# Two cross-attentions written out as one stage of eight head groups, on one Trainium2 core

## The reference, cut to what matters

```python
def _cross_attention(q_in, kv_in, wq, bq, wk, bk, wv, bv, wo, bo, bias_k, bias_v):
    qh = (q_in @ wq + bq).reshape(b, q_len, H, K)          # q_in = layer_norm(x), H = 16, K = 128
    kh = (kv_in @ wk + bk).reshape(b, t, H, K)             # t = 64
    vh = (kv_in @ wv + bv).reshape(b, t, H, K)
    kh = concatenate([kh, bias_k]); vh = concatenate([vh, bias_v])
    logits = einsum('bqhk,bthk->bhqt', qh, kh) / sqrt(K)
    ctx = einsum('bhqt,bthk->bqhk', softmax(logits), vh)
    return ctx @ wo + bo
x = x + _cross_attention(layer_norm(x), ctx, ...)   # l0a
x = x + _cross_attention(layer_norm(x), ctx, ...)   # l0b
```

## Time and profile before

| | us |
|---|---|
| median of 3 runs | 3078.57 (3074.22 to 3082.83) |
| profiled execution | 3079.7 |
| its span, first to last instruction | 3077.9 |
| the stages of the change: 0 to the MLP's first instruction | 882.9 |
| PE busy, whole span | 2784.8 (90%) |
| DVE busy | 1447.1 (47%) |
| ACT busy | 840.4 (27%) |
| granted TensorE clock, mean | 0.950 |

### The profile page before, as it was taken

How to read it: one execution, slowest core, us unless ns; L and a number is a source line. 1 busy time by engine, 2 the same in 40 slices (tenths; PEclk the granted TensorE clock), 3 DMA queues, 4 the chain that set the end, 5 groups by cost and what they waited for, 6 DMA issues and landing times. The chain is left out here.

```text
span 3077.9 us, 31096 instructions
## 1 busy us (share of the span) xinstructions
PE 2784.8 (90%) x11800; PEld 1970.5 (64%) x11800; DVE 1447.1 (47%) x2189; ACT 840.4 (27%) x1598; POOL 406.6 (13%) x234
## 2 busy tenths in 40 slices
PE   6999978999969999979999999859999788779999
PEld 4777656777748888744544444348888444468887
DVE  3554474455475434234535354354343545374443
ACT  4133314332332111212535352431111122241110
POOL 2000002000012000012424253322000300040000
PEclk9999989999979999979999999889999899989999
DMA  3111011101010000202212212030000101110001
GB/s 122 55 55 55 1 60 56 32 24 55 0 60 14 28 14 1 110 7 55 55 52 51 56 48 56 22 126 28 14 14 1 62 28 62 48 59 28 28 1 55
DMA packets 60097, 130.65 MB, mean 42 GB/s; under 512 B 30673, under 2 KB 30802, under 8 KB 49234
## 3 DMA queue, kind: packets, MB, share of 16 engines
q1 hardware_dynamic: 43218, 128.61, 12.3%
q10 hardware_dynamic: 16768, 0.53, 0.3%
HBM read 83.03 MB, written 8.45 MB: 30 GB/s over the span
## 5 line engine op out<-in xcount | busy, mean ns | idle before, releaser
L1268 ACT ACTIVATE l_weighed<-l_across 128x512 f32<-128x512 f32 (+1 forms) x320 | 183.0, 595 | 297.2 <-PE l_across L1151 293.5
L1318 DVE TENSOR_REDUCE l_top<-l_slot 128x1 f32<-128x512 f32 x256 | 170.4, 679 | 189.4 <-PE l_slot L1129 188.7
L999 POOL TENSOR_TENSOR l_paired<-l_weighed 128x2048 f32<-128x2048 f32 x32 | 145.6, 4549 | 393.5 <-ACT l_weighed L1268 333.5
L1151 PE MATMUL l_across<-l_q_stack,l_k_stack 99*128 99x512 f32 (+1 forms) x320 | 185.7, 585 | 12.2 <-ACT l_weighed L1268 9.2
L475 PE MATMUL l0a_wide<-l0a_key_map,l0a_norm 128*128 128x260 f32 x512 | 118.7, 385 | 9.3 <-DVE l0a_soft L630 7.2
L475 PE MATMUL l0b_wide<-l0b_key_map,l0b_norm 128*128 128x260 f32 x512 | 118.7, 385 | 9.3 <-DVE l0b_soft L630 7.2
L1129 PE MATMUL l_slot<-l_k_stack,l_q_stack 97*128 97x512 f32 x256 | 111.9, 438 | 12.9 <-DMA l_k_stack<-l_k_parts 6.6
L1151 PEld LDWEIGHTS l_across<-l_q_stack,l_k_stack 99*128 99x128 f32 (+1 forms) x320 | 59.0, 186 | 96.9 <-issue 61.8
L1837 ACT ACTIVATE l2m_hidden<-l2m_up,columns 128x512 f32<-128x512 f32 x64 | 44.2, 692 | 270.4 <-PE l2m_up L131 268.9
L1837 ACT ACTIVATE l0m_hidden<-l0m_up,columns 128x512 f32<-128x512 f32 x64 | 44.1, 691 | 269.8 <-PE l0m_up L131 268.1
L1837 ACT ACTIVATE l3m_hidden<-l3m_up,columns 128x512 f32<-128x512 f32 x64 | 44.1, 691 | 268.6 <-PE l3m_up L131 266.9
(11 more groups left out here) (423 smaller groups left out, 6313.5 us busy)
## 6 DMA issues: line engine op xcount, KB each, us to landing
l_k_stack<-l_k_parts SPq DMA_DIRECT2D x192, 72.0 KB, 2.0
l_q_stack<-l_q_parts SPq DMA_DIRECT2D x192, 64.0 KB, 2.0
l0m_raw<-in_weights SPq DMA_DIRECT2D x8, 1024.0 KB, 4.8
l2m_raw<-in_weights SPq DMA_DIRECT2D x8, 1024.0 KB, 6.0
l3m_raw<-in_weights SPq DMA_DIRECT2D x8, 1024.0 KB, 4.8
x<-in_x SPq DMA_DIRECT2D x4, 1024.0 KB, 8.6
l0a_wk<-in_weights SPq DMA_DIRECT2D x4, 1024.0 KB, 5.2
l0a_wv<-in_weights SPq DMA_DIRECT2D x4, 1024.0 KB, 7.0
```

Of the source, the lines that this page charges most:

```text
L999: pool.tensor_tensor(paired[:, :, :], weighed[:, first % RING, :, :], weighed[:, (first + 1) % RING, :, :], ALU.add)\
L1151: pe.matmul(across[0:height(c), use % 2, :], k_stack[0:LAST, g % 2, j, keys_of(c)], q_stack[0:LAST, g % 2, j, :], start=True, stop=True).t ...
L1268: act.activation(weighed[0:height(c), (CHUNKS * g + c) % RING, j, :], across[0:height(c), use % 2, :], ACT.Exp)\
L1318: dve.tensor_reduce(top[:, t, j:j + 1], slot[:, i % 2, :], AX.X, ALU.max, negate=True).then_inc(s["top_ready"], 1)
```

## The change

The load stage, both norm stages and both attention stages become one stage, `l0_attentions`, whose eight groups (G = 0 to 7; group g = G % 4 of attention a = G // 4) are written out in Python without a hardware loop. In it

- the inputs and the first weights are issued at once, in the order context, wk, columns, wv, x of batch 0, wo, x of batch 1, wq, x of batches 2 and 3;
- the norm is computed inside groups 0 and 4: `moments`, `scale_rows` on DVE, `turn_norm` on PE between the query tiles and between logits tiles, `take_norm` on ACT;
- five of the next group's eight key and value projections are written before and behind `turn(G, 3)`;
- a value map tile holds one batch and is made by four matmuls of 32 stationary columns each, into four different 32-partition quarters of a bank; the learnt value's tile likewise. ACT copies a tile once, as the high part, and DVE subtracts it from the PSUM bank for the low part;
- the keys hold the learnt key behind each batch (260 columns), so that one copy takes a query tile;
- the logits are read in two halves of two tiles each, and the next logits tile waits only for its own half;
- the learnt value and the output bias come in as one more matmul in each output tile of the last group (`stack_T`, `learnt_map`), whose stationary side is made by `turn_stack`. The closing part, its 16 adds, the trips to DRAM and POOL's bias adds go.

Core of the diff (new code; what it replaces is printed above):

```diff
+            def map_values(G):
+                pe.wait_ge(s["wo_loaded"], 16 * (G + 1))
+                for pair in range(HG // 2):
+                    ...
+                    for b in range(B):
+                        out = prep_bank(G, OUT_TILE + B * pair + b)
+                        for part in range(4):
+                            h, at = 2 * pair + part // 2, b * C + part % 2 * 32
+                            last = pe.matmul(out[32 * part:32 * part + 32, :], values[:, h, at:at + 32], wo[:, h, :], start=True, stop=True)
+                        last.then_inc(s["prep_done"], 1)
+            def turned_bank(use):
+                i = USE[use]
+                if i >= 2:
+                    pe.wait_ge(turned_out[i % 2], i // 2)
+                return turned[:, i % 2, :]
+            def logits_tile(G, b, j):
+                ...
+                if b:
+                    pe.wait_ge(s["logits_read"], 2 * (G * B + b - 1) + j // 2 + 1)
+                else:
+                    pe.wait_ge(prep_out[j], prep_outs(G, BIAS_TILE + j))
+            def out_tile(G, b, j):
+                ...
+                if learnt:
+                    last = pe.matmul(added[:, j % 2, :], stack_T[:, b % 2, tokens], learnt_map[:, :], start=False, stop=True)
+                last.then_inc(s["out_done"], 1)
+            for G in range(ALL):                                   # PE
+                a, first = G // GROUPS, G % GROUPS == 0
+                if G == 0:
+                    project(G, 0, range(HG))
+                    project(G, 1, (0,))
+                project(G, 1, (1, 2, 3))
+                map_values(G)
+                for k in range(KT):
+                    for h in range(HG):
+                        map_query(G, k, h)
+                        if first and h % 2 == 0:
+                            turn_norm(a, k // 2, (k % 2) * 2 + h // 2)
+                map_learnt(G)
+                map_bias(G)
+                for j in range(TPB):
+                    logits_tile(G, 0, j)
+                for j in range(TPB):
+                    logits_tile(G, 1, j)
+                    if first:
+                        turn_norm(a, 2, j)
+                turn(G, 0)
+                for b in (2, 3):
+                    for j in range(TPB):
+                        if j == TPB - 1:
+                            turn(G, b - 1)
+                        logits_tile(G, b, j)
+                        if j == 0 and b == 2:
+                            turn_stack(G, 0)
+                        if j == TPB - 1:
+                            turn_stack(G, b - 1)
+                        if j:
+                            out_tile(G, b - 2, j - 1)
+                        if j == TPB - 1 and first and b == 2:
+                            turn_norm(a, 3, 0)
+                            turn_norm(a, 3, 1)
+                    out_tile(G, b - 2, TPB - 1)
+                    if first and b == 2:
+                        turn_norm(a, 3, 2)
+                        turn_norm(a, 3, 3)
+                for j in range(TPB):
+                    out_tile(G, B - 2, j)
+                if G + 1 < ALL:
+                    project(G + 1, 0, (0, 1))
+                turn(G, B - 1)
+                if G + 1 < ALL:
+                    project(G + 1, 0, (2, 3))
+                    project(G + 1, 1, (0,))
+                turn_stack(G, B - 1)
+                for j in range(TPB):
+                    out_tile(G, B - 1, j)
...
+                if first:                                          # ACT, start of a group
+                    roots(a, 0)
+                    roots(a, 1)
+                take_values(G, (1, 2, 3))
+                take_map(G)
...
+                if first:
+                    roots(a, 2)
+                    roots(a, 3)
+                take_bias(G)
+                if first:
+                    for k in range(KT):
+                        take_norm(a, 2, k)
+                exps(G, 0)
...
+            def normalise(G, b):                                   # DVE
+                ...
+                dve.tensor_tensor(probs...).then_inc(s["probs_ready"], 1)
+                here = learnt_all[:, b * TPB:(b + 1) * TPB, :, :]
+                link(dve.tensor_tensor(here[:, :, :, g], ...), g == GROUPS - 1)
+                if g == GROUPS - 1:
+                    ...
+                    link(dve.tensor_copy(mine[:, :, :, 0:GROUPS].bitcast(F32R), here), False)
+                    link(dve.tensor_copy(mine[:, :, :, AGAIN:AGAIN + GROUPS].bitcast(F32R), here))
+                    dve.tensor_tensor(mine[:, :, :, LOW:LOW + GROUPS], here, mine[:, :, :, 0:GROUPS], ALU.subtract).then_inc(s["stack_ready"], 1)
...
+                if first:                                          # DVE, start of a group
+                    scale_rows(a, 0)
+                    scale_rows(a, 1)
+                    moments(a, 2)
+                    take_map(G, range(4))
+                    moments(a, 3)
+                    take_map(G, range(4, 8))
+                else:
+                    take_map(G, range(8))
+                add_learnt(G)
...
+                shift(G, 3, lambda step: add_outs(G, 1, 2 + step, 3 + step))
+                if last and G + 1 < ALL:
+                    moments(a + 1, 0)
+                add_outs(G, 2, 0, 2)
+                normalise(G, 3)
+                split_probs(G, 3)
+                add_outs(G, 2, 2, TPB)
+                if last and G + 1 < ALL:
+                    moments(a + 1, 1)
+                add_outs(G, 3, 0, TPB)
```

More of the change, by code:

```diff
@@ new lines, in kind, with take_keys @@
+            def kind(G, name, count=1, h=0):
+                at = COLUMNS[f"{tag_of(G)}_{name}"] + HG * (G % GROUPS) + h
+                return n.columns[:, at:at + count]
+            def take_keys(G, heads):
+                for h in heads:
+                    bank = prep_bank(G, KEY_TILE + h)
+                    if h == 0:
+                        act.copy(keys[:, :, :, C], kind(G, "bias_k", HG).unsqueeze(2).to_broadcast([P, HG, B]))
+                    act.activation(keys[:, h, :, 0:C], bank[:, 0:CTOK].rearrange("p (b c) -> p b c", b=B), ACT.Identity,
+                                   bias=kind(G, "bk", 1, h)).then_inc(prep_out[h % TPB], 1)
@@ new lines, in take_values, with take_map @@
+            def take_values(G, heads):
+                for h in heads:
+                    act.activation(values[:, h, :], prep_bank(G, VALUE_TILE + h)[:, 0:CTOK], ACT.Identity,
+                                   bias=kind(G, "bv", 1, h)).then_inc(prep_out[h % TPB], 1)
+            def take_map(G):
+                if G:
+                    act.wait_ge(s["out_done"], TPB * B * G)
+                for i in range(OUT_TILE, QUERY_TILE):
+                    pair, b = (i - OUT_TILE) // B, i % B
+                    act.copy(map_hi[:, pair, b, :], prep_bank(G, i)).then_inc(s["map_high"], 1)
@@ L1965, in build @@
         n = Net(nc, ctx, dram)
-        for stage in (load_stage, *STAGES):
+        for stage in STAGES:
             stage(n)
```

741 lines of the change are left out of this document (405 added, 336 removed).

## The result

The changed kernel took 2958.3 us (median of 4 runs, 2953.5 to 2959.4) where the kernel before took 3076.4 (median of 4): a ratio of 0.961, 95% interval 0.960 to 0.962. That is 118 us less; 109 were forecast, and the time lies 12 us under the forecast and inside its range. The profiled execution took 2953.5 us with a span of 2951.7.

A forecast was written before the change was run, and what follows sets the result against it. PE's own work was taken as most of a group, its gaps as what can be had. Start, eight groups and end summed to 774 us against 882.9, so 3078.6 - 109 = 2970 us; range 2947 to 3005.

The forecast's parts named there:

- The steady group: Groups 1, 2, 5 and 6: shorter waits and work take 11.0 us off 97.8, leaving 86.8 us.
- The value map's form: Four 32-column matmuls a set on PE: 0.94 us a set by the trace, against 1.09 by the skill's efficiency.
- Rival 1: Value map: the four 32-column matmuls follow one another, 3.5 us a set, +182, 3152 us; chance 3%.
- The start: Before group 0's first logits: DVE's moments, rows and map tiles are the chain; first logits at 48.8 us instead of 75.77.
- Groups 0 and 4: Price of the norm beside the work: +13.5 us behind the first logits, and +6.2 before group 4's queries.
- the lower clock after the idle: Groups 0 and 4, behind PE's 6.5 us idle at the first turning: slower matmuls cost 2.6 us.
- Groups 3 and 7: Closing products, transposes and waits of the learnt rows and bias: group 3 takes 100 us, group 7 91.9.
- +5.0: Group 7, which projects nothing: it keeps the waits and lower clock around the last turning, 5.0 us.
- the last stack copy: Groups 3 and 7: a wait of 0.9 us for it before batch 3's outputs.
- rival 4: Steady groups: written-out code has fewer register waits and they reach PE's work of 84 us; 2948 us; chance 8%.
- rival 2: Clock and hand-offs: each clock loss doubled (about +12) and 3 us more in each group; 3005 us; chance 15%.
- rival 3: The norm is not hidden, as x lands late or DVE's order starves PE; 3020 us; chance 4%.

The follow-up runs named there:

- one-quarter kernel: Changed kernel with all four 32-column matmuls of a value-map set written to output partitions 0 to 31 in groups 1 to 7: 3112.3 us.
- no-norm run: Changed kernel without the second attention's normalisation, which reads the first's normalised x instead: 2945.2 us, block's end 741.5.
- the projections back: Changed kernel with the next group's key and value projections put back at the head of each group: 2989.7 us, 0.971 of the kernel before.
- the moments late: Changed kernel with the second attention's batch 0 moments moved on DVE behind the normalising of group 3's batch 3: 2958.1 us, block's end 761.3.
- the value map first: Changed kernel with DVE taking all eight value-map tiles before the moments of batches 2 and 3 in groups 0 and 4: 2964.4 us, block's end 760.5.

## Why the prediction was right, step by step

**The steady group**: forecast 86.8, measured 86.7, by terms of which two were off and cancelled; that it came to 0.1 us is luck. The value map takes 7.00 us, not 7.8: the sets run at 0.875, not at the mean of the earlier trace rows, and the bank is never waited for. Query and bias tiles take 9.3, not 8.7: at 0.47 each they don't reach the pace of the logits, 0.433, which I had given them. Projections 13.7 (13.8), learnt value 1.00 (0.95), logits to turning 14.4 (14.65), turning to output 5.1 (5.15), the long stretch 29.5 (29.3), turning and outputs 6.7 (6.5). The 11 us saved are counted from the group of the earlier trace rows, which has the largest drop of clock of its kernel: its 2.8 us are in one other of the eight groups, four have 1.5 to 1.7, and two have none behind the same idle of 2.16 us. So the forecast 5.2 for moving the projections holds 2.8 of clock that not every group had; by experiment the move is worth 3.0 us and 1.6 more where the clock falls. The half reads are shown as 1.6 (forecast 1.1). The 2.5 of the learnt value are read off the rows, 3.53 in the earlier trace rows and 1.00 now; the other shares were not tried apart.

**The value map's form.** The trace has 0.875 us a set, a full f32 matmul of 512 columns by the 0.86 of one matmul in the one-quarter kernel (27.58 / 32). Four column quarters side by side gain 3.9 times over one after another. The Trainium skill ("TensorE: Matmul & The Clock Gate", Part 3) has a gain of 2.38 times for three column tiles, from which the prediction's estimate of 1.09 us a set was worked out; the measurement decides against it. Rival 1 (3152) describes what happens when all four write one quarter, and that kernel is slower than the one before.

**The start**: first logits at 47.9, forecast 48.8, by the chain that was named. DVE's moments, rows and map tiles follow each other (the two halves of the map tiles start at 28.14 and 33.53, for 28.7 and 34.5), and PE waits for them twice, 1.27 and 1.74 us. Taking the map first gave 3.0 us there.

**Groups 0 and 4**: first turning 22.0 us after the first logits (forecast 22.1), PE idle for 6.07 (6.5). ACT's order as the cause is shown by the edit that removes it. The sums were 1.6 and 3.0 us too dear. The normalisation costs 16.8 us in group 4 (no-norm run), where the terms came to 13.5 + 6.2 = 19.7. Ahead of its first logits it costs 5.1, not 6.2: the queries start 14.1 us behind the last output, not 15.1, and 0.5 of the 6.2 has no term (2.2 + 3.5 is 5.7). Behind them it costs 11.7, not 13.5, and there the mis-sized term is the lower clock after the idle, put at 2.6: from the first turning to the first output it is 6.29 and 6.01 us in groups 0 and 4 for 5.09 in a steady group, so 1.2 and 0.9. A wait of 0.49 us that a steady group has there vanished in the slower rows. The other terms came out: 7.6 for 7.5, and 3.2 for the 3.35 of rows, transposes and the last norm copy.

**Groups 3 and 7.** Group 3: 98.8 for 100, the moments' wait 2.36 for 3.0, and 1.5 for the clock (97.3 us in the execution that has the wait and no drop) for 1.5. The stack is 1.83 + 0.83 of waiting, for 2.4 + 0.9. The step that was off most is group 7, with the end 89.7 us for 93.8. Its +5.0 carried a drop of the clock, 2.8 us in the earlier trace rows, over to the last turning. In the profiled execution the idle comes there as 0.20, 1.11 and 0.83 us with transposes between, and the clock stays. That is not a rule of this place: of eleven executions that have the idles of 1.11 and 0.83 there, the clock fell in four (the projections back, the one quarter, the moments late, the value map first) and cost some 1.5 us each time. So the term was a chance of 1.5 us, taken as a sure 2.8. The rest of the 4.1 us are waits counted twice: "the last stack copy" stands inside the wait that the +5.0 already holds. The closing costs 5.0 to 6.5 us a group by experiment, not 8.7.

**The sum.** Block's end 762.8 for 774: start 0.9, group 0 1.6, groups 1 and 2 0.2, group 3 1.2, group 4 3.0, groups 5 and 6 0.2, group 7 4.1. That is 11 of the 12 us by which the median lies under the forecast. The stages behind were taken as unchanged, and took 2188.9 us for 2195.0 in the profiled executions, within the 7 us by which two executions of one kernel differ there. The time lies halfway to rival 4 (2948), but not by its mechanism: steady groups stayed at 86.7, not 84. Of rival 2 no doubled loss of clock came, and no steady group lost 3 us more; of rival 3 nothing came.

## What to carry to other kernels

A seam between stages is dearer than its work: here three of them held 102 of the 120 us, at a clock of 0.66 to 0.91, while PE was at 94% inside the groups. When a small job is folded into a tuned stage, look at each engine's queue for the place where it stands ahead of something PE waits for: three such places, one on ACT and two on DVE, had left 24 us, and moving a few lines got them. And compare small edits by the end of the stage that they touch; the whole time of a single run had the wrong sign for one of them. Even the stage's end holds luck: each drop of the clock that comes in one execution and not in the next moved it by 0.7 to 1.6 us, so look at the rows behind each idle before you give a microsecond to the edit.

## What the hardware showed that I had not expected

- Behind an idle of about 2 us the clock fell in most places, not in all, and not in the same ones in every kernel. Of 23 idles of 2.16 to 2.36 us in front of a group's products, 17 are followed by matmuls at 1.2 GHz (7 of 8 of 2.36 us, 4 of 7 of 2.31, and 6 of 8 of 2.16 in the kernel before), for a cost of some 1.5 to 2.8 us, and 6 by none. Idles of 1.11 and 0.83 us with 0.63 of transposes between had it in 4 of 11 executions. Whether cutting an idle in two helps is not shown by so few. That work moved into an idle saves the idle, and with it the chance of the drop, is: behind the last turning of the changed kernel's steady groups there is neither.
- A set of column parts that fill the array costs one full f32 matmul of 512 columns whatever its parts: 0.875 us for four of 32, 0.878 for two of 64, 3.45 for four of 32 in one quarter.
- Stages whose code is the same took 2188.9 to 2202.1 us in profiled executions of different kernels, and 2188.9 and 2195.7 in two of the same one, with a clock a little lower for some hundred microseconds. A gain of a few microseconds can't be seen in the whole time of one run.
